# Capture of the row maxima in pieces of one operand, the mean of the keys in three steps, and wider spacing in the selection of queries

## What is computed

```python
scores = jnp.einsum('bhqd,bhkd->bhqk', q, k) * scale          # 4096 x 4096 per head
sparsity = scores.max(axis=-1) - scores.mean(axis=-1)
_, top_idx = jax.lax.top_k(sparsity, U)                        # U = 307
q_sel = jnp.take_along_axis(q, top_idx[..., None], axis=2)
attn = jax.nn.softmax(jnp.einsum('bhud,bhkd->bhuk', q_sel, k) * scale, axis=-1)
out = jnp.zeros_like(q).at[bi, hi, top_idx].set(jnp.einsum('bhuk,bhkd->bhud', attn, v))
x = _layernorm(x + out.reshape(b, l, D) @ Wo + bo)
# then: mix each token with the one before, r = sigmoid(xr W_r^T), k = relu(xk W_k^T)^2,
# x = _layernorm(x + r * (k W_v^T))
```

## Time and profile before

| | us |
|---|---|
| median of 3 runs (lowest to highest) | 3242.62 (3241.13 to 3245.9) |
| profiled execution | 3246.53 |
| its span, first to last instruction | 3244.8 |
| DVE busy | 2894.6 |
| PE busy | 2945.3 |
| ACT busy | 2821.5 |
| POOL busy | 1611.0 |
| last slot of the main loop ends | 2942.7 |
| mean granted TensorE clock | 0.976 of full |

### The profile page before, as it was taken

The page is one execution under the profiler, slowest core; times in us unless marked ns, Lnnn a source line. Parts: engine busy times, 40 slices in busy tenths (PEclk is TensorE's granted clock), DMA queues, the critical chain, the costliest instruction groups (busy, mean ns, idle before and its releaser), DMA issues. The chain is left out here.

```text
span 3244.8 us, 56078 instructions
## 1 busy us (share of the span) xinstructions
PE 2945.3 (91%) x14524; PEld 1334.2 (41%) x14524; DVE 2894.6 (89%) x5704; ACT 2821.5 (87%) x6214; POOL 1611.0 (50%) x2867
## 2 busy tenths in 40 slices
PE   6999899998999999999899999899998799897588
PEld 3333333333433433443343444444444343344376
DVE  4999999999989998998999999899998698997567
ACT  5999898998999999999899888799997699895476
POOL 4223022224645554653364566766546464657754
PEclk8999999999999999999999999999999999998889
DMA  6324223241251242123111252122241212202122
GB/s 183 92 84 119 74 72 86 86 41 34 44 42 29 37 42 36 21 39 36 35 37 44 51 46 51 38 39 36 42 48 38 46 33 20 42 17 16 19 84 74
DMA packets 276909, 166.61 MB, mean 51 GB/s; under 512 B 182188, under 2 KB 256108, under 8 KB 272492
## 3 DMA queue, kind: packets, MB, share of 16 engines
q1 hardware_dynamic: 268492, 159.56, 26.0%
q0 software_dynamic: 6144, 1.37, 0.5%
q10 hardware_dynamic: 1952, 2.10, 0.2%
HBM read 111.86 MB, written 47.86 MB: 49 GB/s over the span
## 5 line engine op out<-in xcount | busy, mean ns | idle before, releaser
L1185 DVE CUSTOM_DVE_ANT_0 JK<-DP,AB 128x1024 bf16<-128x1024 f32 x2048 | 2459.6, 1222 | 215.2 <-DVE SPr L1185 88.6
L1035 ACT ACTIVATE AB<-CP 128x512 f32<-128x512 f32 x4096 | 2292.1, 623 | 188.5 <-PE CP L782 131.1
L801 PE MATMUL DP<-KS,QS 128*128 128x512 f16 x4096 | 1233.5, 383 | 69.1 <-DVE SPr L1185 60.8
L1673 POOL TENSOR_TENSOR SCR<-E 128x307 f16<-128x307 f32 x957 | 665.1, 708 | 491.4 <-ACT E L1064 485.4
L782 PE MATMUL CP<-KS,QS 128*128 128x512 f16 x2048 | 791.4, 386 | 56.3 <-ACT AB L1035 33.0
L791 PE MATMUL CP<-KS,QS 128*128 128x512 f16 x2048 | 792.2, 387 | 36.3 <-ACT AB L1035 0.2
L801 PEld LDWEIGHTS DP<-KS,QS 128*128 128x128 f16 x4096 | 354.4, 99 | 368.7 <-DVE SPr L1185 179.1
L1064 ACT ACTIVATE E<-BP 128x307 f32<-128x307 f32 x896 | 428.5, 478 | 40.3 <-PE BP L862 34.4
L782 PEld LDWEIGHTS CP<-KS,QS 128*128 128x128 f16 x2048 | 197.6, 96 | 532.8 <-ACT AB L1035 457.9
L791 PEld LDWEIGHTS CP<-KS,QS 128*128 128x128 f16 x2048 | 196.8, 96 | 421.1 <-ACT AB L1035 375.2
L862 PE MATMUL BP<-QT,KA 128*128 128x307 f16 x896 | 265.7, 297 | 12.4 <-DMA QT<-SCR 8.6
(11 more groups left out here) (411 smaller groups left out, 3016.9 us busy)
## 6 DMA issues: line engine op xcount, KB each, us to landing
KS<-KTC SPq DMA_DIRECT2D x256, 128.0 KB
QS<-QSC SPq DMA_DIRECT2D x512, 64.0 KB
KA<-KTC SPq DMA_DIRECT2D x128, 128.0 KB
QN<-SCR SPq DMA_DIRECT2D x16, 544.0 KB, 3.4
SCR<-in_L_attn_x SPq DMA_DIRECT2D x16, 512.0 KB, 5.1
AO<-E SPq DMA_DIRECT2D x16, 512.0 KB, 6.8
VF<-in_L_attn_x SPq DMA_DIRECT2D x64, 128.0 KB, 2.1
VF<-AO SPq DMA_DIRECT2D x64, 128.0 KB, 2.2
```

The costliest lines, as they stand in the source:

```text
L801: r = pe.matmul(o[:, 512 * j:512 * j + 512], qs, ks[j][:, 0, :], start=True, stop=True)
L1035: act.activation(AB[p % 3][:, 512 * j:512 * j + 512], BANK["C%d" % j], ACT.Abs).then_inc(ab_full, 1)
L1185: dve.tensor_tensor_reduce(out=JK[p % 2][:], in0=BANK["D%d" % u], in1=AB[p % 3][:], scale=1.0, scalar=0.0, op0=ALU.add, op1=ALU.max, accum ...
L1673: pool.tensor_tensor(EL[a % NE], E[a % NE][:], EH[a % NE], ALU.subtract).then_inc(el_g, 1)
```

## The change

Four edits.

1. **Capture.** It is now a step for each quarter, ("cap", g, c), put behind slots 15, 31, 47 and 63 of the group's last head. DVE reduces the pair u = 0, 1 of a quarter with one TENSOR_REDUCE into the first of the three copies; POOL makes the other two from it, and `flip` waits for POOL's semaphore cap_pool. L1243 (the threshold of the next digit) becomes a TENSOR_SCALAR with one tensor and two column scalars.
2. **Mean of keys.** kbar is split into xbar (DVE), kbar (PE) and kadd (DVE); in batch 1 they are three and four slots apart, in batch 0 they stay in one step.
3. **Spacing in the selection.** Before rank 3 empty steps in place of 1, or 7 while feed of batch 0 runs; between pick and slots 3 (5 during feed) in place of 2.
4. **Spacing in the prelude.** 5 empty steps ahead of the gather, 3 in place of 5 between it and arr, 2 in place of 4 behind; qt of the group's first head is issued there, ahead of attend, if the group before has ended its attention.

```diff
 def tokens(b, fast):  (not fast)
-            yield [("kbar", b, bank())]
+            yield [("xbar", b)]
+            yield []
+            yield []
+            bk = state["late"] = bank()
+            yield [("kbar", b, bk)]
+            yield [("kadd", b, bk)]
+            state["late"] = None
 def select(g):
         for i in range(5):
             yield [("cum", g, i, "D" if tail[0] else "G")]
-        for _ in range(gaps):
+        for _ in range((7 if "feed" in done and "f0" not in done else 3) * gaps):
             yield []
         yield [("rank", g, bank())]
         for _ in range(gaps):
             yield []
         yield [("pick", g, "D" if tail[0] else "G")]
-        for _ in range(2 * gaps):
+        for _ in range((5 if "feed" in done and "f0" not in done else 3) * gaps):
             yield []
         yield [("slots", g)]
 def prelude(g):
+        for _ in range(5 * gaps):
+            yield []
         yield [("gath", g, 0)]
-        for _ in range(5 * gaps):
+        for _ in range(3 * gaps):
             yield []
         state["arranged"] += 1
         yield [("arr", g, 0)]
-        for _ in range(4 * gaps):
-            yield []
+        for _ in range(2 * gaps):
+            yield []
+        if g == 0 or g - 1 in done:
+            state["turned"].add(HEAD0[g])
+            yield [("qt", g, 0)]
+            yield []
+        yield []
         ahead.add(g)
 main loop of the plan
             plan.append(("main", n * NP + p))
+            if n + 1 in HEAD0 and p % 16 == 15:
+                plan.append(("cap", HEAD0.index(n + 1) - 1, p // 16))
...
-            plan.append(("cap", g))
 PE, flip
-                pe.wait_ge(cap, g + 1)
+                pe.wait_ge(cap_pool, 4 * (g + 1))
 DVE
-            def kbar(b, bank):
+            def xbar_(b):
                 q = seq.mark(dve.reduce_sum(xbar[:], xpart[:], mybir.AxisListType.X))
                 dve.wait_ge(q_dve, q)
                 dve.tensor_scalar(xbar[:], xbar[:], 1.0 / L, None, ALU.mult).then_inc(kb_dve, 1)
+
+            def kadd(b, bank):
                 dve.wait_ge(wsplit, 1)
...
-                dve.wait_ge(rowmax, NP * HEAD0[g + 1])
-                for c in range(NT // NQ):
-                    first, second = (SPr[:, NQ * c:NQ * c + NQ, 0:n, u].rearrange("p t h -> p h t").unsqueeze(2).broadcast_to(
-                        [128, n, NJ, NQ]) for u in range(2))
-                    r = dve.tensor_tensor(SV[g][:, c], first, second, ALU.max)
-                r.then_inc(cap, 1)
+                dve.wait_ge(rowmax, NP * (HEAD0[g + 1] - 1) + 16 * (c + 1))
+                dve.tensor_reduce(SV[g][:, c, :, 0, :], SPr[:, NQ * c:NQ * c + NQ, 0:n, :].rearrange("p t h u -> p h t u"),
+                                  mybir.AxisListType.X, ALU.max).then_inc(cap, 1)
...
-                dve.scalar_tensor_tensor(out=to, in0=hits[0:rows, 15:16], scalar=ahead_of[0:rows, i:i + 1],
-                                         in1=limits_of(i)[0:rows, 1:2], op0=ALU.add, op1=ALU.add).then_inc(sel_lim, 1)
+                dve.tensor_scalar(to, limits_of(i)[0:rows, 1:2], hits[0:rows, 15:16], ahead_of[0:rows, i:i + 1], ALU.add,
+                                  ALU.add).then_inc(sel_lim, 1)
 POOL
+            def capture(g, c):
+                n = GROUPS[g][2]
+                pool.wait_ge(cap, 4 * g + c + 1)
+                pool.tensor_scalar(SV[g][:, c, :, 1:NJ, :], SV[g][:, c, :, 0:1, :].broadcast_to([128, n, NJ - 1, NQ]), 1.0, 0.0,
+                                   ALU.mult, ALU.add).then_inc(cap_pool, 1)
```

More of the change, by code:

```diff
@@ L116, in product @@
                 if fast and hi and c == 0:
-                    yield [("kbar", b, bank())]
+                    bk = bank()
+                    yield [("xbar", b), ("kbar", b, bk), ("kadd", b, bk)]
         def splits(c):
@@ L581, in attention_rwkv @@
         val_pe, val_act, val_pool = (sem(n) for n in ("val_pe", "val_act", "val_pool"))
-        sc_c, sc_d, ab_full, rowmax, cap = (sem(n) for n in ("sc_c", "sc_d", "ab_full", "rowmax", "cap"))
+        sc_c, sc_d, ab_full, rowmax, cap, cap_pool = (sem(n) for n in ("sc_c", "sc_d", "ab_full", "rowmax", "cap", "cap_pool"))
         sel_thr = sem("sel_thr")
@@ L1179, in main @@
                 hl = n - HEAD0[g]
-                if (hl, t, u) == (0, 0, 0):
-                    after(dve, cap, g)
+                if g and (hl, t % NQ, u) == (0, 0, 0):
+                    dve.wait_ge(cap, 4 * (g - 1) + t // NQ + 1)
                 after(dve, rowmax, p - 1)
@@ L1203, in views @@
                 return [q[:].rearrange("p t h -> p (t h)")[:, 0:NT * n] for q in (slotf, sloti, slb)]
+            def capture(g, c):
+                n = GROUPS[g][2]
+                if g > 1 and c == 0:
+                    dve.wait_ge(sel_m, 4 * (g - 1))
+                    dve.wait_ge(l_m, 64 * HEAD0[g - 1])
+                dve.wait_ge(rowmax, NP * (HEAD0[g + 1] - 1) + 16 * (c + 1))
+                dve.tensor_reduce(SV[g][:, c, :, 0, :], SPr[:, NQ * c:NQ * c + NQ, 0:n, :].rearrange("p t h u -> p h t u"),
+                                  mybir.AxisListType.X, ALU.max).then_inc(cap, 1)
             def parts(g):
@@ L1434, in f9 @@
                                       ALU.mult).then_inc(f_o3, 1)
-            stages = dict(xtev=xtev, kbar=kbar, kev=kev, split=split, main=main, cap=capture, parts=parts, cmp=cmp,
+            stages = dict(xtev=xtev, xbar=xbar_, kadd=kadd, kev=kev, split=split, main=main, cap=capture, parts=parts, cmp=cmp,
                           digit=digit, cut=cut, cum=cum, rank=rank, pick=pick, slots=slots, ob=ob, oa=oa, idx=idx,
@@ L1784, in f9 @@
                     pool.tensor_scalar(fo[k % 4], fo[k % 4], r[:, 0:1], r[:, 1:2], ALU.mult, ALU.add).then_inc(f_o3, 1)
-            stages = dict(vset=vset, vev=vev, vones=vones, qzero=qzero, split=split, cut=cut, cum=cum, pick=pick, slots=slots, ob=ob, qgzero=qgzero, gath=gath, arr=arrange,
+            stages = dict(vset=vset, vev=vev, vones=vones, qzero=qzero, cap=capture, split=split, cut=cut, cum=cum, pick=pick, slots=slots, ob=ob, qgzero=qgzero, gath=gath, arr=arrange,
                           st=st, put=put, f1=f1, f2m=f2m, f2r=f2r, f3=f3, f5=f5, f6k=f6k, f7=f7, f8=f8, f9=f9)
@@ L1873, in sel @@
                     sp.wait_ge(l_q, 128 * (b + 1))
-                    sp.wait_ge(cap, g + 1)
+                    sp.wait_ge(cap, 4 * (g + 1))
                 c0 = (h0 + h) * (DH + 1) + DH
```

5 lines of the change are left out of this document (removed).

## The result

The changed kernel takes 3222.0 us, median of 5 runs (3215.7 to 3228.8), beside 3243.7 us for the kernel before: ratio 0.9932, 95% interval 0.9911 to 0.9953, so it is about 22 us faster. The forecast was 3205 us, 37.7 us faster, with a range from 3190 to 3224. The sign and the range held, the size did not: two fifths of the expected gain are missing. The same kernel timed again later (e9) gave nearly the same ratio, 0.9928 (0.9911 to 0.9946), so the gap is not a matter of few runs.

What follows compares the result with a forecast made beforehand. No single engine bounds the kernel: PE, DVE and ACT take turns, and time goes where slots take far longer. Main loop 30.7 + tail 7 = 37.7 us off 3242.6 gives 3205 us, range 3190 to 3224.

Steps and rivals of the forecast that it cites:

- Captures: Main-loop captures: shorter one-operand pieces save 10 us (6 to 13); POOL's copies cost 2 us (0 to 11).
- Mean of keys: Batch 1's mean of keys: DVE no longer waits inside the stage, saving 3.5 us (2 to 5).
- Sums and rank of group 5: Six more slots before group 5's rank cover POOL's late running sum, saving 4.5 us (1 to 5.5).
- QT: Transposed queries of (5, 0), issued early ahead of key loads: PE's wait goes whole, saving 10 us (7 to 11).
- Gather of (5, 0): Five further slots cover POOL's wait for indices; 2 us left for its DMA issues; saving 6 us (3 to 8).
- Gather of (4, 0): Group 4's gather moves to one place before the mean f2m, costing 1.3 us (0 to 3).
- Feed's changed alignment: Feed's nine-slot pattern meets the search at other places; a few us allowed in the range.
- Tail: Behind slot 2047: shorter captures and threshold, steps moved to the main loop; 7 us saved (2 to 12).
- A: Rival: removed waits return as POOL's lateness; 19 us less than summed, 3223 us; chance 0.15.
- B: Rival: one-operand threshold and reductions still stall beside POOL; tail gives 2, captures 5, 3215 us; chance 0.15.
- C: Rival: slower, as POOL's 32 new waits hold up ACT and PE; 3253 us at 1.5 us each; chance 0.03.
- D: Rival: all POOL's tail slack is usable; 12 in the tail, 4 more in the main loop, 3196 us; chance 0.15.

Runs made afterwards that it cites:

- e9: The changed kernel timed once more, with no edit: 3220.1 us, ratio 0.9928 to the kernel before.
- e1: The kernel before with the captures alone in one-operand reductions and POOL's copies, no spacing: 3231.0 us, ratio 0.9972.
- e3: The kernel before with the threshold (L1243) alone computed by TENSOR_SCALAR with one SBUF tensor: 3235.0 us, ratio 0.9989.
- e2: The kernel before with the mean of keys alone split into its three steps: 3233.1 us, ratio 0.9979.
- e5: The kernel before with only feed of batch 0 beginning 4 slots later: 3238.6 us, ratio 0.9980.
- e10: The changed kernel with the transposed queries of head (5, 0) issued late, at slot 1794: 3227.7 us, ratio 0.9949 to the kernel before.
- e8: The changed kernel with the edits of e6 and e7, and the gather of (5, 0) behind feed's last mix: 3215.9 us, ratio 0.9903 to the kernel before.
- e7: The changed kernel with the gather of (4, 0) behind the mean f2m of its slot: 3214.3 us, ratio 0.9898 to the kernel before.
- e6: The changed kernel with feed's loads put ahead of the QS and KS loads directly preceding them: 3216.8 us, ratio 0.9904 to the kernel before.
- e4: The kernel before with the spacing alone (rank, pick, gather prelude, early transposed queries): 3234.2 us, ratio 0.9985.
- e12: The changed kernel with each captured piece written by three DVE reductions, no POOL copy: 3221.4 us, ratio 0.9932 to the kernel before.

## Why the prediction was right in sign and wrong in size

**Captures**: right. 10 less 2 was forecast; e1 has 9 us as a time, and its main loop is 7.2 us shorter than e3's. The 2 us charged to POOL were a guess near the truth: the one place that pays in e1 costs 2.3 us.

**Mean of keys**: right. 3.5 forecast, 3.9 in the slots behind it, in e2 4.3.

**Sums and rank of group 5**: the size was right (4.5, measured 4.3 to 6.2), the cause half. PE's wait at the running sum is gone, but e5 without any spacing already has 2.9 us of it, by the shift of feed.

**QT**: right, 10 forecast and 9.2 measured, undone by e10. What I did not see is that the loads ahead are half of the cause: with feed four slots later QT still stands behind them, and the wait is gone (e5).

**Gather of (5, 0)**: this step failed, 6 us forecast, -1.2 measured (+0.8 between the first traces of both kernels). The step was "so I leave 2 us" for the squares and mixes behind the three issues. POOL's wait for the indices is gone as forecast, but POOL then has no gap to put 3.8 us of issues in: the last mixes end 3.24 us late for PE, and slot 1785 takes 5.42 us. With the gather behind the last mix (e8) DVE's wait there falls from 4.18 to 1.56 us. The wait that was removed had hidden the issues' cost.

**Gather of (4, 0)**: the mechanism was right, "one place before the mean f2m", but the term was mis-sized: +1.3 (0 to 3) against 5.0 at slots 1440 to 1472. The row of 2.56 us that I took it from was of a place where the issues had a slot of lead. Less than half of the 5.0 is the gather's place: with it behind the mean (e7) 1.8 to 2.4 us come back, and the rest stays as POOL's lateness at the next tile.

**The step that was missing**: that the spacing moves other work past borders of SP's queue. The text said of QT that it must not stand behind the key loads, and did not ask the same of feed's loads, though feed begins four slots later. Tile 5's load went behind the 16 issues: 4.2 us net, shown by e5 and e6. "Feed's changed alignment" was in the range but in no term.

**Slots 1920 to 1952**: 2.7 us more, in no term. In both traces of the changed kernel a TENSOR_SCALAR with one source is stalled there while POOL converts, as it is, shorter, in e3 (1.88 us):

```profile
2769.45 2.88 DVE L1333 TENSOR_SCALAR SCR<-fb 128x96 f16<-128x96 f16 x1
```

It is the second trace; in the first one it takes 2.86 us; both stand at slot 1938, e3's at 1934. Which alignment makes it longer stays open.

**Tail**: right in size, 7 forecast and 6 measured; the parts are not as forecast. The three edits alone have tails that are 2.2 (e1), 4.4 (e3) and 7.1 us (e4) shorter than the mean of the unedited ones, 13.7 in sum. The spacing, to which the forecast gave 1.3 us, alone reaches what all three have together, though in its trace the thresholds still take 9.2 us for 12. So the match of the 7 is in part luck. The forecast charged the loss to POOL, and POOL is busy most of the time, 39.29 of 46.10 us right behind the last slot (columns as in rows 8, whose 39.73 us begin 4.2 us behind it; right behind its last slot the kernel before has 37.61):

```profile
2930.40:2976.50 46.10, 34.43 (x180) 18.39 (x180) 23.68 (x90) 20.90 (x49) 39.29 (x62) 0.78 0.65 16
```

That POOL makes the loss is argued from these shares; no experiment shows it.

**The rivals.** A, which gave 3223 us, came nearest to the time, and the trace bears out its mechanism in three of the four new stalls. But its 19 us are mis-added: rank 1, gather 3, tail 2 and captures 6 are 13.5 to 15.5 us less than the sum (as the captures stand for 8 or 10), so it says 3219 to 3221 us. Rank (4.3 to 6.2), tail (6) and captures (7 to 9) were better than these, the gather (-1.2) worse, and it has no term for feed's load; that it lands so near is luck too. Its counter-argument, "POOL is busy half the span", is the flaw: that is the page's mean. From 1850 to 2090 us, where feed and search meet, POOL was busy 155 of 240 us already before, and in the changed kernel from 2005 to 2100 it is (PE, PE's loads, DVE, ACT, POOL):

```profile
2005.00:2100.00 95.00, 79.03 (x372) 41.04 (x373) 78.84 (x168) 65.04 (x142) 67.32 (x153) 0.95 0.20 43
```

71%. B fell by e3 and by the 32 short reductions, C by e12, and D by the time. Of the signs named in advance, the last slot ends at 2930.0 us and not at 2912. POOL's waits for S grew from nothing to 70.8 us, far beyond the 10 that were to mean "wrong", and cost at most some 5 us (e12): the sign was bad, as in e1. ACT's wait for the mean grew from 24.0 us to 28.7, less than the 10 us that I had set, though two waits of over 4 us in it cost DVE as much: the sum over all tiles hides them. "The freed slots show a new wait of the same size" caught 1785 and, at 4.27 us for 7.46, slot 1733, and missed 1287, 1411 and 1460.

## What to carry to other kernels

Spacing added to one in-order chain moves all that waits for its end. Before trusting a removed stall, list for every moved DMA what stands ahead of it in its queue, before and after; here 16 loads at a head's border cost 4 to 9 us where a needed transfer came right behind them (f0 in e5, QT of (1, 0) in e4, QT of (5, 0) in e10), nothing where it came 4.8 us behind (QT in e5), and putting the needed one ahead returned it (e6). Read an engine's slack in the stretch in question, not on the page: work taken off a wait has to be done somewhere, and where the engine has no idle time, moving the work may only move the wait (the gather of (5, 0), at each of three places). And where parts of a change shift each other, the sum of the parts' times can agree with the whole (9 + 7 + 4 + 5 = 25 us, measured 22) while each part's account is another one.

## What the runs showed of the hardware

Whether DVE was stalled beside a busy POOL depended on the instruction's form. Forms with two SBUF tensors were stalled up to 4.8 us (SCALAR_TENSOR_TENSOR of one element, rows 8; TENSOR_TENSOR of 192 f16 elements, 4.79 us above). The one-source TENSOR_SCALAR of 96 f16 elements was stalled too, 2.88 us against 0.18, and so was that of two f32 elements (xbar in the setup, 3.22 us in the changed kernel, 3.59 before, against 0.17). The one-source reduction of f32 (32 executions, 202 to 239 ns) and TENSOR_SCALAR with one f32 element and two scalars (0.27 us) never were. The Trainium skill (Advanced Engine Details and Errata, VectorE Performance Modes) says that GpSimd instructions and Vector instructions in a two-port mode block each other, and gives the even or equal odd dimensions that such a mode asks for; its table has such modes for tensor_scalar and none for tensor_tensor or tensor_reduce. The trace agrees for one source: the 96 elements of f16 and the two of f32 fit and were stalled; the threshold's single element with one tensor does not fit and was not, nor were the 32 reductions, so rival B's condition for them did not hold. The stalls of forms with two SBUF tensors are no case of this rule; they are what the traces show.

Such a stall can outlast many of POOL's instructions. In the kernel before, POOL around 2793.7 us, where the 4.79 us stand:

```profile
2793.72 0.71 POOL L1673 TENSOR_TENSOR SCR<-E 128x307 f16<-128x307 f32 x1
2794.38 0.65 POOL L1621 TENSOR_TENSOR SCR<-SCR,tokc 128x96 f16<-128x96 f16 x2
2794.99 0.69 POOL L1673 TENSOR_TENSOR SCR<-E 128x307 f16<-128x307 f32 x1
2795.65 0.65 POOL L1621 TENSOR_TENSOR SCR<-SCR,tokc 128x96 f16<-128x96 f16 x2
2796.27 2.77 POOL L1673 TENSOR_TENSOR SCR<-E 128x307 f16<-128x307 f32 x4
```

Ten instructions follow each other without a gap, from 2793.72 to 2799.04, and DVE's one ends at 2798.49, just after the ninth ends and while the tenth runs. The two thresholds of 4.80 and 4.59 us end in the same way, 0.01 to 0.02 us after the seventh of eight conversions. But xbar in the setup ends with the first of two MEMSETs that follow each other without a gap (3.22 us). So in these four the end lies within 0.25 us of the end of a POOL instruction; at which one of a run it comes stays open. Whether such a run meets such an instruction was chance in these traces (in 1 of 4 with that order), and beside the start of the first slot it is the largest difference that I found between profiles of one order. Whether these two make the spread of the runs (6 to 21 us for one kernel) was not tested.
